# Cross-attention over 25088 tokens: the remainder of 512 first, one order for every later superstep

## The reference

```python
# x: 256 tokens x 512; ctx: 25088 tokens x 512
q  = layernorm(x) @ wi;  kp = vp = ctx @ wi              # wi: 512 x 64
head = q + softmax(q @ kp.T / 8) @ vp                    # one softmax over all 25088 tokens
x = x + tile(head, 16) @ Wo + bo                         # Wo: 1024 x 512
x = x + attention_layer(layernorm(x))    # q, k, v: softmax(h @ K.T) @ V over 512 learned rows each,
                                         # 16 causal heads, an output layer of the same kind,
                                         # then one over 2048 rows (fK, fV)
x = x + mixture(layernorm(x))            # 8 experts, the best 2 of each token
```

## Time and profile before

| | |
|---|---|
| median of 3 runs | 549.9 us (549.8 to 550.41) |
| profiled execution | 548.89 us, of which the span of the trace is 547.2 us |
| granted TensorE clock, mean | 0.983 |
| TensorE matmul busy | 507.7 us (93%) |
| VectorE busy | 419.8 us (77%) |
| ScalarE busy | 328.7 us (60%) |
| DMA | 122.45 MB, mean 224 GB/s |

### The profile page before, as it was taken

One profiled execution on the slowest core, in us unless ns is written; L12 is line 12 of the kernel. 1 busy time (PEld: TensorE's weight loads), 2 busy tenths in 40 slices (PEclk: granted clock), 3 DMA queues, 4 the chain that ended last, 5 costly groups with the idle time before them and its releaser, 6 DMA issues.

```text
span 547.2 us, 11166 instructions
## 1 busy us (share of the span) xinstructions
PE 507.7 (93%) x4243; PEld 346.1 (63%) x4243; DVE 419.8 (77%) x709; ACT 328.7 (60%) x640; POOL 34.5 (6%) x105
## 2 busy tenths in 40 slices
PE   5989999999999997689998889898799999999995
PEld 1334544454454454479866777687688888888885
DVE  2377778777877786968575876998888998998994
ACT  2445544554454445556474646876577788778772
POOL 2000001111110100000312000000000000000000
PEclk9999999999999997899999999999899999999999
DMA  8999888889987400516420402558777987986001
GB/s 332 335 359 397 318 325 322 324 320 334 380 337 261 174 1 2 198 37 237 146 78 1 153 2 105 211 211 333 293 239 283 383 313 255 372 311 225 0 2 41
DMA packets 35937, 122.45 MB, mean 224 GB/s; under 512 B 2609, under 2 KB 2609, under 8 KB 31282
## 3 DMA queue, kind: packets, MB, share of 16 engines
q1 hardware_dynamic: 35602, 121.27, 59.5%
q10 hardware_dynamic: 288, 0.52, 0.3%
HBM read 121.26 MB, written 0.52 MB: 223 GB/s over the span
## 4 chain that ended last, share of the span: by engine, by line
PE 45%; DVE 11%; ACT 4%; issue 2%; DVEq 0%; POOL 0%; ACTq 0%
PE score_banks L1084 15%; PE bank L1120 7%; PE score_banks L662 2%; PE score_banks L713 2%; DVE w_split L1874 2%; PE score_banks L862 2%; PE bank L1093 1%; PE bank L672 1%; PE score_banks L886 1%; PE score_banks L1009 1%; PE bank L862 1%; PE bank L662 1%; PE bank L536 1%; ACT w_split L1396 1%; ACT arena L1401 1%
## 5 line engine op out<-in xcount | busy, mean ns | idle before, releaser
L1166 ACT ACTIVATE xprobs<-score_banks,small 128x512 f32<-128x512 f32 (+1 forms) x104 | 67.9, 664 | 97.9 <-DVEq L1606 69.3
L1731 DVE TENSOR_TENSOR w_split<-arena,w_split 128x1024 fp32r<-128x1024 f32 x96 | 114.0, 1219 | 7.0 <-ACT w_split L1297 5.1
L1297 ACT ACTIVATE w_split<-arena 128x1024 fp32r<-128x1024 f32 x96 | 100.7, 1060 | 15.3 <-PE score_banks L1084 9.9
L490 PE MATMUL bank<-arena,wi_sb 128*64 128x512 f32 (+1 forms) x400 | 91.5, 598 | 6.4 <-DMA arena<-in_ctxT 6.4
L1084 PE MATMUL score_banks<-w_split,xg 128*128 128x512 f32 x384 | 88.8, 390 | 1.0 <-issue 1.0
L1615 DVE STREAM_TRANSPOSE xprobsT<-xprobs 128x1024 f32<-128x1024 f32 (+1 forms) x52 | 61.6, 1184 | 34.1 <-ACT xprobs L1166 32.7
L1084 PEld LDWEIGHTS score_banks<-w_split,xg 128*128 128x128 f32 x384 | 71.7, 188 | 16.9 <-ACT xg L1466 1.3
L1587 DVE TENSOR_REDUCE small<-score_banks 128x2 f32<-128x1024 f32 (+1 forms) x52 | 57.2, 1137 | 14.0 <-PE score_banks L521 14.0
L490 PEld LDWEIGHTS bank<-arena,wi_sb 128*64 128x64 f32 x400 | 26.6, 138 | 54.7 <-issue 53.2
L521 PE MATMUL score_banks<-k_full,hT 64*32 64x256 f32 (+1 forms) x1664 | 49.9, 371 | 5.1 <-ACT xprobs L1166 3.9
L536 PE MATMUL bank<-xprobsT,v_rows 128*64 128x256 f32 x392 | 48.5, 390 | 0.0
(11 more groups left out here) (315 smaller groups left out, 734.3 us busy)
## 6 DMA issues: line engine op xcount, KB each, us to landing
arena<-in_ctxT SPq DMA_DIRECT2D x23, 2048.0 KB, 8.8
arena<-in_w12T SPq DMA_DIRECT2D x32, 1024.0 KB, 5.1
arena<-in_w3T SPq DMA_DIRECT2D x16, 1024.0 KB, 5.6
arena<-in_fKT SPq DMA_DIRECT2D x4, 1024.0 KB, 7.3
arena<-in_fV SPq DMA_DIRECT2D x4, 1024.0 KB, 5.1
arena<-in_ctxT SPq DMA_DIRECT2D x4, 512.0 KB, 6.1
arena<-in_Wo SPq DMA_DIRECT2D x1, 2048.0 KB
arena<-in_kKT SPq DMA_DIRECT2D x1, 1024.0 KB, 11.0
```

The lines of the kernel that those rows point to most:

```text
L490: last = pe.matmul(kp_bank[b][DH * h:DH * (h + 1), 0:half], wi_sb[:, k, :], ctx_buf[:, b, k, h * half:(h + 1) * half], start=(k == 0), sto ...
L1166: act.activation(xprobs[:, qb, 0:2 * width].rearrange("p (h n) -> p h n", h=2), score_banks[:, 2 * p:2 * p + 2, 256 * q:256 * q + width], ...
L1297: act.activation(w_split[:, i % 4, 0, :], raw, ACT.Copy).then_inc(part_high, 1)
L1731: return dve.tensor_tensor(w_split[:, i % 4, 1, :], raw, w_split[:, i % 4, 0, :].bitcast(F32), ALU.subtract)
```

## The change

Positions below are in tokens; `LAST` stays 12.

- **Remainder first.** Superstep 0 has the 512 tokens alone, in a place of its own (`ctx_small`, slot 0 of the arena, free until `kK` is loaded there). Supersteps 1 to 12 are full. Since the remainder lies in neither of the two buffers, blocks 1 and 2 are issued without waiting; from block 3 on SyncE waits for `kp_done` as before.
- **Start.** TensorE: keys of the remainder, q, `turn_keys(0)`, keys of block 1, scores 0, keys of block 2, scores 1, both `turn_keys`; then a superstep 1 without `turn_o` whose `pv(0)` is short.
- **Superstep 10** has Wo's fold behind its first scores, and ScalarE's copies of it ahead of its first exponentials. (The loads of Wo are issued behind block 6.)
- **Superstep 11** has the query part of the output behind its first scores, both calls of `pv(10)` ahead of its second, `turn_o(9)` and `turn_o(10)`, and at its end the first query tile of `pv(11)` as `pv_rows`. VectorE adds the query part to x behind its first maxima.
- **Superstep 12**, now a full one: scores, `pv_rows(11)` for tile 1, `turn_o(11)`, 12 `keep_awake`, scores, and then for each tile: `pv_rows(12)`, the accumulator turned, and the product with Wo as two accumulating matmuls (one for the last `o`, one for the accumulator). Maxima differences, fades and copies are made tile by tile.
- **Denominators** are summed over the quadrants by a matmul with a new constant, `quads`, made by GpSimd at the start (one memset, seven selects), in place of eight small VectorE operations.
- **Next layer.** `kK`'s two halves go to a place of their own (`kK_split`), cut within superstep 12; the order of scores is k0, q0, k1, q1 in place of k0, k1, q0, q1, and the work of ScalarE and VectorE there is set to it.

```diff
             for n in range(1, STEPS + 1):
-                b, width = n % 2, STEP if n < STEPS else 2 * HALF0
-                if n >= 2:
+                b, at = n % 2, SMALL + (n - 1) * STEP
+                if n >= 3:
                     sp.wait_ge(kp_done, n - 1)
...
-                if n == 5:
+                if n == 6:
                     sp.dma_start(wo_sb, Wo.rearrange("(g p) n -> p g n", p=P)).then_inc(wo_in, 16)
...
+            def pv_rows(u, par, st, dst):
+
+                pe.wait_ge(probs_turned, 4 * u + 2 * st + 2)
+                pe.wait_ge(v_done, 2 * u + 1)
+                if st == 0:
+                    pe.wait_ge(o_out, u)
+                nt = HALF // P
+                for part in range(2):
+                    for j in range(nt):
+                        for h in range(2):
+                            block = (2 * h + part) * nt + j
+                            last = pe.matmul(dst[DH * h:DH * (h + 1), :], v_rows[par][:, part, j * P + DH * h:j * P + DH * (h + 1)],
+                                             xprobsT[par][:, 4 * st:4 * st + 4, 32 * block:32 * (block + 1)],
+                                             start=(part == 0 and j == 0), stop=(part == 1 and j == nt - 1))
+                return last
...
-            turn_keys(0, 0, 0)
-            pe.wait_ge(ctx_in[1], 16)
-            kp(1, 1, HALF)
+            turn_keys(0, 0, 0, HALF0, 1)
+            next_keys(1, 0)
             pe.wait_ge(ev("q_high"), 1)
-            scores(0, 0, 0)
-            turn_keys(0, 0, 1)
-            next_keys(1, 0)
-            scores(0, 0, 1)
+            scores(0, 0, 0, 1, HALF0)
             next_keys(1, 1)
+            scores(0, 0, 1, 1, HALF0)
             turn_keys(1, 1, 0)
             turn_keys(1, 1, 1)
-            superstep(1, 1)
-            for u in range(2, LAST - 1):
+
+            scores(1, 1, 0)
+            next_keys(2, 0)
+            scores(1, 1, 1)
+            next_keys(2, 1)
+            pv(0, 0, 0, 1, HALF0)
+            turn_keys(2, 0, 0)
+            turn_keys(2, 0, 1)
+            for u in range(2, LAST - 2):
                 superstep(u, u % 2)
 
+            scores(LAST - 2, 0, 0)
+            pe.wait_ge(ev("wo_summed"), len(wo_sums))
+            pe.wait_ge(consts_done, MADE["fold"])
+            pe.wait_ge(v_done, seen(LAST - 2, 0))
+            pe.matmul(kp_bank[0], fold[:], wo_sum, start=True, stop=True).then_inc(ev("wo_folded"), 1)
+            turn_o(LAST - 4)
+            pv(LAST - 3, 1, 0)
+            pe.wait_ge(ev("wo_dup_ready"), 2)
+            next_keys(LAST - 1, 0)
+            scores(LAST - 2, 0, 1)
+            next_keys(LAST - 1, 1)
+            pv(LAST - 3, 1, 1)
+            turn_keys(LAST - 1, 1, 0)
+            turn_keys(LAST - 1, 1, 1)
+
             scores(LAST - 1, 1, 0)
...
+            turn_o(LAST - 3)
+            pv(LAST - 2, 0, 0)
+            pv(LAST - 2, 0, 1)
+            scores(LAST - 1, 1, 1)
+            pe.wait_ge(ev("q_added"), 1)
+            next_keys(LAST, 0)
+            turn_o(LAST - 2)
+            pe.wait_ge(ev("q_added"), 2)
+            next_keys(LAST, 1)
+            pv_rows(LAST - 1, 1, 0, of_bank[:, 0:P])
+            turn_keys(LAST, 0, 0)
+            turn_keys(LAST, 0, 1)
+
+            scores(LAST, 0, 0)
+            pv_rows(LAST - 1, 1, 1, of_bank[:, P:T]).then_inc(o_ready, 1)
             turn_o(LAST - 1)
-            pv(LAST, 0, 0, 1, HALF0)
...
+            pe.wait_ge(v_done, seen(LAST, 1))
+            pe.wait_ge(ev("mask_ready"), 2)
+            keep_awake(kp_bank[0], 12)
+            scores(LAST, 0, 1)
...
+            pv_rows(LAST, 0, 0, of_bank[:, 0:P]).then_inc(o_ready, 1)
+            turn_acc(0)
+            project(0, kp_bank[1])
+            keep_awake(kp_bank[0], 8)
+            pe.wait_ge(denom_done, LAST + 1)
+            pe.wait_ge(consts_done, MADE["quads"])
+            pe.matmul(SB[1][:, 0:QB], quads[:], denom, start=True, stop=True).then_inc(ev("denom_summed"), 1)
+            pv_rows(LAST, 0, 1, kp_bank[0][:, 0:P]).then_inc(o_ready, 1)
+            turn_acc(1)
+            project(1, SB[3])
...
-            keep_awake(SB[0], 8)
             turn_rows(hln, [T6, T7], "h", [0])
-            keep_awake(SB[0], 6)
+            keep_awake(SB[0], 5)
...
             scores_of("k", 0)
             turn_rows(hln, [T6, T7], "h", [1])
+            scores_of("q", 0)
             scores_of("k", 1)
-            scores_of("q", 0)
             turns_of("k", 0)
```

ScalarE and VectorE, the parts that the prediction speaks of:

```diff
-            values_out(0, 0, 0)
-            keys_out(0, 0, 1)
-            values_out(0, 0, 1)
-            soft(0, 0, 0)
+            act.wait_ge(keys_turned, 1)
+            act.activation(v_rows[0][:, 0, 0:HALF0], kp_bank[1][:, 0:HALF0], ACT.Copy).then_inc(v_done, 1)
             keys_out(1, 1, 0)
-            soft(0, 0, 1, (0,))
+            soft(0, 0, 0, width=HALF0 // 4)
             keys_out(1, 1, 1)
-            soft(0, 0, 1, (1,))
             values_out(1, 1, 0)
             values_out(1, 1, 1)
+            soft(0, 0, 1, width=HALF0 // 4)
...
+            soft(LAST - 1, 1, 0)
+            o_copy(LAST - 2)
+            soft(LAST - 1, 1, 1, (0,))
+            keys_out(LAST, 0, 0)
+            soft(LAST - 1, 1, 1, (1,))
+            fade_out(LAST - 1)
             attn_high("kK")
+            keys_out(LAST, 0, 1)
+            values_out(LAST, 0, 0)
+            values_out(LAST, 0, 1)
...
+            soft(LAST, 0, 1)
+            last_fade(1)
+            act.activation(warm, eps_col, ACT.Sqrt)
+            last_o(1, kp_bank[0][:, 0:P])
...
             for st in range(ST):
                 layer_norm_std("h", st)
+                attn_high("qK", st, st + 1)
                 hT_out("hT", (T6, T7), [st])
...
             soft_max("k", 0, B[0])
+            soft_max("q", 0, B[2])
+            soft_norm("k", 0)
+            attn_low("vK", 0, 1)
             soft_max("k", 1, B[1])
-            soft_norm("k", 0)
+            soft_norm("q", 0)
+            probsT_low("k", 0)
+            attn_low("vK", 1, 2)
             soft_norm("k", 1)
-            attn_low("vK")
-            soft_max("q", 0, B[2])
-            probsT_low("k", 0)
             soft_max("q", 1, B[3])
-            soft_norm("q", 0)
+            probsT_low("k", 1)
             soft_norm("q", 1)
```

More of the change, by code:

```diff
@@ L398, in _ @@
                       allow_small_or_imprecise_dtypes=True).then_inc(consts_done, 1)
+            pool.memset(quads[:], 0.0).then_inc(consts_done, 1)
+            for n in range(7):
+                pool.wait_ge(consts_done, MADE["slot_id"] + 1 + n)
+                pool.affine_select(out=quads[:], in_=quads[:], compare_op=ALU.not_equal, fill=1.0, base=32 * (n - 3),
+                                   pattern=[[-1, P]], channel_multiplier=1).then_inc(consts_done, 1)
             def denominators(u, b, first=False):
@@ L603, in _ @@
             turn_keys(1, 1, 1)
-            superstep(1, 1)
-            for u in range(2, LAST - 1):
-                superstep(u, u % 2)
-            scores(LAST - 1, 1, 0)
-            turn_o(LAST - 3)
-            next_keys(LAST, 0, HALF0)
-            pv(LAST - 2, 0, 0)
-            scores(LAST - 1, 1, 1)
-            pe.wait_ge(ev("wo_summed"), 7)
-            pe.wait_ge(consts_done, MADE["fold"])
-            pe.wait_ge(v_done, 2 * LAST)
-            pe.matmul(kp_bank[1], fold[:], wo_sum, start=True, stop=True).then_inc(ev("wo_folded"), 1)
@@ L631, in _ @@
                           stop=True).then_inc(ev("xattn_ready"), 1)
-            turn_o(LAST - 1)
-            pv(LAST, 0, 0, 1, HALF0)
-            pe.wait_ge(ev("acc_faded"), 1)
-            for st in range(ST):
-                last = pe.transpose(turned_bank[:, T + st * P:T + (st + 1) * P], acc[:, st, :], ident[:])
-            last.then_inc(ev("acc_turned"), 1)
-            pe.wait_ge(ev("o_total"), 1)
-            for st in range(ST):
-                pe.matmul(SB[2 + st], o_sb[:, st * P:(st + 1) * P], wo_dup, start=True, stop=True).then_inc(ev("xattn_ready"), 1)
+            turn_o(LAST - 3)
@@ L653, in split_tile @@
                 g = 2 * SPLIT_UNITS.index(unit) + n // 2
-                return [w_split[:, g % 4, part, (n % 2) * 512:(n % 2 + 1) * 512] for part in range(2)]
+                return [split_home(g)[:, part, (n % 2) * 512:(n % 2 + 1) * 512] for part in range(2)]
             def key_scores(m, st, bk):
@@ L1662, in _, with attn_low @@
             superstep(3, 1)
-            with dve.Fori(4, LAST, 2) as u:
+            def attn_low(unit, first=0, stop=2):
+                for g, home, raw in list(halves(unit))[first:stop]:
+                    dve.wait_ge(ev("attn_high"), g + 1)
+                    dve.tensor_tensor(home[:, 1, :], raw, home[:, 0, :].bitcast(F32),
+                                      ALU.subtract).then_inc(ev("attn_low"), 1)
+            with dve.Fori(4, LAST - 2, 2) as u:
                 superstep(u, 0)
@@ L1678, in _ @@
-            last.then_inc(ev("acc_faded"), 1)
+            superstep(LAST - 2, 0)
+            chunk_max(LAST - 1, 1, 0)
```

(25 more changed lines are left out.)

252 lines of the change are left out of this document (150 added, 102 removed).

## The result

The changed kernel takes 544.45 us (median of 4 runs, 542.02 to 546.02) against 549.85 (549.06 to 550.41) for the kernel before on the same chip: ratio 0.9897, 95% interval 0.9872 to 0.9921. Run again on another chip it took 544.47 (6 runs), ratio 0.9905, interval 0.9882 to 0.9927. The forecast was 546.6 in a range of 544.0 to 550.0: the sign and the range held, but the gain is 5.4 us where 3.3 stood.

What follows compares the result with a forecast made beforehand. TensorE bounds the steady supersteps, with open time only at the ends; seven terms, −9.7 − 0.85 + 0 + 1.0 + 5.6 + 0.45 + 0.25, sum to −3.25, so 546.6 us against 549.9, range 544.0 to 550.0.

Steps and rivals of the forecast that it cites:

- Term 1: Start to superstep 1's first scores: smaller first load lands block 1 sooner; 24.9 us, 9.7 less.
- Rival B: Start: blocks 1 and 2 share the DMA engines, superstep 1 starts near 28.4; +3.5, 550.1 us, chance 0.08.
- Term 2: Superstep 1: loses a turn and most of pv, bound by the chain; 14.95 us, −0.85.
- Term 3: Supersteps 2 to 9: same instructions in the same order; 126.5 us, no change.
- Term 4: Superstep 10: Wo's fold stands where TensorE has no gap; 16.8 us, +1.0.
- Term 5: Superstep 11: now full, with query part, one more turn_o and first pv_rows; 20.2 us, +5.6.
- Term 6: Superstep 12 to first key scores: full chain, 0.75 put in for a clock fall; 24.3 us, +0.45.
- Term 7: First key scores to first features: q0 ahead of k1 saves standing, k1's turn about 0.95 late; 20.7 us, +0.25.
- rival A: Clock stays up and bounds fall well at start, superstep 1 and key phase: 544.0 us, chance 0.12.
- Rival C: Narrow pv_rows matmuls cost 1.8 at each of two places, or k1's turn 2.2 more: 548.8 to 550, chance 0.12.
- D: Rival: clock falls during the last exponentials, stays at 0.50 for 6.6 us; +4.3 over forecast, 550.9, chance 0.07.
- E: Rival: order has no effect, only TensorE's total work counts; 549.9 us, chance 0.06.

Runs made afterwards that it cites:

- e8: Changed kernel plus nine unused identity matmuls on TensorE from about 2.3 us, before the first context arrives: 544.99 us, ratio 0.9918.
- e4: Changed kernel with block 2 asked for only when the remainder's keys are done, instead of at once: 548.12 us (one run).
- e6: Changed kernel with Wo's fold and the query part moved into superstep 12 in place of 12 keep_awake, kK and key copies reordered: 543.09 us, ratio 0.9877.
- e11: Kernel before with every longer gap from 205 to 231 us filled by unused products: 547.60 us, ratio 0.9950.
- e3: Kernel before with 12 keep_awake matmuls in the 1.96 us gap ahead of superstep 12's scores: 547.89 us, ratio 0.9962.
- e1: Changed kernel with 20 keep_awake in place of 8 ahead of the denominators' matmul in superstep 12: 543.20 us, ratio 0.9883.

## Why the prediction was right in kind and short in size

Step by step, as it was written:

- **Term 1, start, −9.7: −9.0.** The mechanism holds (e8: the blocks' bytes set the time; e4: with block 2 asked for later it falls apart). Mis-sized by 0.75: both blocks land 0.45 later than 1.05 MB at 412 GB/s gave, and 0.27 is TensorE, still at work at half pace when block 2 was there (18.52 and 18.25). I had read 15.24 as the landing alone; TensorE's work before it ended at 15.29 too. From block 2's keys to superstep 1 it is 7.13 us, where I had 7.1. Rival B, that the two loads share the engines, is refuted: they land 5.1 us apart. What I had not seen is the opposite danger of e4.
- **Term 2, −0.85: −0.78. Term 3, 0: −0.15.** As forecast.
- **Term 4, fold, +1.0: +0.9.** Shown by e6, which takes it away.
- **Term 5, superstep 11, +5.6: +5.2.** The query part and `pv_rows` stand there in full: `pv_rows` took 1.92 us (I took 1.9, the near bound of 1.83 to 3.7). The Trainium skill's 81 ns a pair (TensorE: Matmul & The Clock Gate, section Back-to-back issue gap) would have made it 2.6; here 32 took 1.92, 60 ns each. I had ScalarE's key copies end the superstep at 20.2; TensorE filled it at 19.82.
- **Term 6, +0.45: +0.8 in the profile, −0.8 without a fall.** This is the step that failed in size. Without a fall it is 23.04 to 23.07 (23.55 forecast), with one 24.65. The 0.5 was gained before the last `pv_rows`: VectorE's last transpose was done at +16.8, not +17.4, and what stands behind it took what I gave it. I priced a fall at 0.75, a mean of two outcomes; it costs 1.6, and in the first profile it came in full, in the second not at all.
- **Term 7, key order, +0.25: +0.23.** The turn of k1 waits 0.70 (0.95 forecast).
- **From the profiled pair to the medians.** I carried the profiled execution's distance from its median over unchanged, −1.0 for the kernel before. For the kernel after it was +1.6, and in its second profile, without the fall at 220 us, +0.2; the two spans differ by 1.3, so the fall is most of it. Why the kernel before was profiled 1.0 under its median is not shown. Its start was early (block 1's keys at 15.24; 16.13 in e11), but e3's was as early (15.36), and that execution lay 2.1 above its median. The falls far behind superstep 12 move a run as well: from the first key scores to the end the same work took 314.1 us in e8's profile, with a granted clock of 1.00 from 360 to 400 us, and 316.5 in the second profile of the kernel after, with 0.91 there. The two distances, −1.0 and +1.6, point in opposite directions, so a difference of 2.9 in one pair stands for 5.4 in the medians.

How the 5.4 splits, from ratios applied to 549.85: before kept awake (e11) 547.1, so falls between 205 and 231 us cost it 2.7; after kept awake (e1) 543.4, falls there cost it 1.0 (544.4). So 3.7 us are the order and 1.7 are falls that the change removed. The intervals of these ratios are 0.8 to 1.1 us to either side, so the split is an estimate; the timelines without a fall give 3.1 to 4.1 for the order. The granted clocks agree with it: in 44 runs beside the experiments the kernel before has a mean of 0.979 to 0.987 each time; the kernel after, in ten, has 0.988 to 1.0, and its quickest runs are those with most of it (0.999: 542.02, 1.0: 542.29; 0.988: 545.35). I had expected the times of its second six runs to follow the clock: they do at the ends (1.0: 542.29; 0.989: 545.76 and 545.99), not run by run between them (0.991: 544.25; 0.992: 544.7).

The median lies outside the forecast's own 545 to 548.5 and nearer to rival A's 544.0. That is in part luck for A: its clock stayed up in some executions only, and of its other terms the start (25.65, not 24.3) and the key phase (+0.23, not −0.7) did not come. I had held it unlikely since the new gap was as long as the two behind which it fell, and called falls rare by the mean of the span; but 0.983 over 547.2 us is 18.6 us at half pace, and that in none of 44 runs of the kernel before the mean passed 0.987 was not to be seen in one profile. Rival C is refuted (the narrow products 60 ns each; k1's turn waits 0.70). D's fall came, but the pace was back to full by 224 us, at a cost of 1.6 and not 5. E is refuted, with 2.4 us more busy time in less time. B's 550.1 lies outside the range as well, which the prediction doesn't say.

Left open: why the clock falls in some executions of the kernel after and not in others with the same gap of 1.5 us. The falls behind 248 us, which both kernels have at changing places (363 to 371, 384 to 399, and the last microseconds), were not tried.

## What to carry to other kernels

Put the short block first, where the chip waits for bytes anyway, and keep the next load queued behind it; a load of 2 MB asked for only when its turn comes lands a median of 8.6 us later here, and the engine stands. A block's 5.1 us at full rate is the distance between two queued loads, not the time from issue to landing. Work that has to go somewhere belongs in the superstep where the chain, not TensorE, is the limit, and the order of the full supersteps is kept there, since its long blocks of products cover the exponentials. When a change removes a gap behind which the clock fell, look at several executions before the price of the fall is fixed: one profile shows it in full or not at all.

## What the runs showed of the hardware

- TensorE's first work runs at half pace, to 12 us in one execution of the kernel after and to 9 in e1 (four turns 1.12 us, later and with the warm-up 0.66), while the column of the granted clock shows 1.00 there. Durations tell it, the column doesn't.
- The clock fell behind standing for 1.96 us in before, and in e3 behind two gaps of 0.71 and 0.86 us with light work between: short gaps are not always safe. Behind the same gap of 1.5 us it fell in two executions and not in three.
- A block of 2.1 MB lands 5.1 us behind another that is queued ahead of it, but a median of 8.6 us after it is asked for, and 10.0 in e4, where it was asked for late and the next load came beside it.
- The same start takes up to 0.9 us longer from execution to execution (block 1's keys at 15.24 to 16.13 with the old start; superstep 1 at 25.24 to 26.16 in the kernels with the new start), and all that follows moves with it. In e11, the longest of the old starts, 0.2 of the 0.9 is the bytes, the rest the pace of TensorE's first work.
